# A two-layer token mixer on one core: order of work in the first phase of its recurrent part, and one gate tile moved to phase 8

## The reference

```python
xn = layernorm(x)
h = xn @ Win.T + bin                             # 512 -> 64 features
for l in range(4):
    y = silu(layernorm(h) * l1w + l1b)
    h = h + sconv(y) * scl                       # decaying complex recurrence over the 1024 tokens
    y = layernorm(h) * l2w + l2b
    h = h + silu(y @ W1.T + b1) @ W2.T + b2      # 64 -> 256 -> 64
s = layernorm(h) * lnw + lnb, then @ Wout.T + bout  # 64 -> 512
g = silu(xn @ W.T + bias + low-rank updates)     # 512 -> 512, folded into one matrix weff
x = x + s * g
```

## Time and profile before

| | us |
|---|---|
| median of 3 runs (lowest to highest) | 686.53 (683.98 to 686.88) |
| the profiled execution, its time | 686.92 |
| its span, first to last instruction | 684.8 |
| block A, to the start of block B | 470.3 |
| phase 0, to TensorE's first `center_rows` | 41.4 |
| phases 1 to 7 | 131.8 |
| phases 8 and 9, to the end of the span | 41.3 |

### The profile page before, as it was taken

The page is one execution under the profiler, slowest core; times in us unless marked ns, Lnnn a source line. Parts: engine busy times, 40 slices in busy tenths (PEclk is TensorE's granted clock), DMA queues, the critical chain, the costliest instruction groups (busy, mean ns, idle before and its releaser), DMA issues. The chain is left out here.

```text
span 684.8 us, 8597 instructions
## 1 busy us (share of the span) xinstructions
PE 626.5 (91%) x2772; PEld 450.5 (66%) x2772; DVE 489.6 (71%) x943; ACT 324.1 (47%) x541; POOL 171.9 (25%) x296
## 2 busy tenths in 40 slices
PE   4797999999999999999999999898499999999785
PEld 4676878888888888888888888466244343434332
DVE  6798897787787787787887877587574544445556
ACT  5679286277277267357357448222233333333420
POOL 1000002002002002001001006966543544443324
PEclk9999999999999999999999999899699999999977
DMA  8811001100100200200200107202000000000014
GB/s 296 295 43 63 0 1 52 42 1 28 64 0 0 92 0 0 92 0 0 92 0 0 63 1 259 89 1 58 6 1 0 1 0 0 1 0 1 0 61 185
DMA packets 17182, 32.32 MB, mean 47 GB/s; under 512 B 3225, under 2 KB 3737, under 8 KB 17153
## 3 DMA queue, kind: packets, MB, share of 16 engines
q1 hardware_dynamic: 17152, 31.97, 13.6%
HBM read 24.62 MB, written 7.34 MB: 47 GB/s over the span
## 5 line engine op out<-in xcount | busy, mean ns | idle before, releaser
L750 DVE TENSOR_SCALAR_CACHE_REDUCE junk_d<-k_buf,cand 128x1376 int8<-128x1376 f32 x56 | 91.9, 1640 | 0.3
L581 ACT ACTIVATE junk_a<-k_buf,cand 128x1376 int8<-128x1376 f32 x56 | 80.5, 1437 | 0.6
L1014 PE MATMUL ps_a<-wd_hi,zt_hi 128*128 128x512 f32 (+1 forms) x176 | 71.8, 408 | 1.9 <-DVE zt_lo L863 1.0
L1729 PE MATMUL ps_b<-arena,xt 128*128 128x512 f32 x128 | 71.6, 670 | 0.0
L562 ACT ACTIVATE s_buf<-ps_a 128x1376 f32<-128x1376 f32 x16 | 21.1, 1320 | 106.0 <-PE ps_a L987 103.6
L1014 PE MATMUL ps_a<-wd_hi,zt_lo 128*128 128x512 f32 (+1 forms) x176 | 69.2, 393 | 0.0
L1014 PE MATMUL ps_a<-wd_lo,zt_hi 128*128 128x512 f32 (+1 forms) x176 | 68.9, 392 | 0.0
L503 POOL TENSOR_TENSOR xres<-xres,gate 128x512 f32<-128x512 f32 x12 | 23.5, 1962 | 144.4 <-DVE gate L870 144.4
L495 POOL TENSOR_TENSOR rstd<-var_eps,expo 128x2 f32<-128x2 f32 x8 | 5.6, 706 | 203.7 <-DVE var_eps L691 203.7
L987 PE MATMUL ps_a<-wg_hi,xt_hi 128*128 128x512 f32 (+1 forms) x192 | 52.7, 383 | 1.8 <-DVE xt_lo L679 1.8
L987 PE MATMUL ps_b<-wu_hi,xt_hi 128*128 128x512 f32 (+1 forms) x192 | 52.3, 381 | 0.0
(11 more groups left out here) (225 smaller groups left out, 1282.6 us busy)
## 6 DMA issues: line engine op xcount, KB each, us to landing
xin<-in_x SPq DMA_DIRECT2D x8, 512.0 KB, 3.7
xres<-in_x SPq DMA_DIRECT2D x8, 512.0 KB, 3.4
out<-arena SPq DMA_DIRECT2D x16, 256.0 KB, 2.0
x_scratch<-xres SPq DMA_DIRECT2D x6, 512.0 KB, 3.1
arena<-x_scratch SPq DMA_DIRECT2D x3, 1024.0 KB, 11.8
m_buf<-in_wd_t SPq DMA_DIRECT2D x3, 512.0 KB, 9.3
m_buf<-in_wg_t SPq DMA_DIRECT2D x2, 688.0 KB, 5.6
k_buf<-in_wg_t SPq DMA_DIRECT2D x2, 688.0 KB, 8.0
```

The costliest lines, as they stand in the source:

```text
L581: act.activation(junk_a[:], k_buf[:, 1, :], ACT.Sign, bias=c, scale=-1.0, accum_out=below[:, 1:2]).then_inc(act_step, 1)
L750: dve.tensor_scalar(junk_d[:], k_buf[:, 0, :], c, -float(DROP), ALU.is_lt, ALU.add, accum_out=e).then_inc(cnt_dve, 1)
L1014: last = pe.matmul(ps_a[:, t, :], zs, ws[0:rows, c, :], start=(c == 0 and n == 0), stop=(c == CHUNKS - 1 and n == 2))
L1729: last = pe.matmul(bankg[k % 2], xt[:, n - 1, t * P:(t + 1) * P], weff[:, n - 1, :], start=False, stop=(n == KH))
```

## The change

On ScalarE, `apply_tokens` now normalizes groups 2 and 3, as scale and bias of an activation; VectorE makes the bias (`negated`, minus mean times inverse root) and normalizes no tile of block B. Six banks serve for the transposes. The statistics of group 3 stand between VectorE's copies. The low part of the bias rows is made for two rows alone, in waits of VectorE (`rows_low`), and the means of `w2` are taken in a wait (`weight_means`), apart from their subtraction (`take_means`). GpSimd takes the first inverse roots ahead of its constants, and makes three tables of a phase instead of two, the third after `widen`. The bias row of a gate tile becomes its last step. In phase 0 one gate tile is made instead of two, and the sixteenth tile lies in phase 8 (`LAST_GATES`). In each phase ScalarE's `gate` of the first tile moves behind both `norm_out`s.

```diff
+LAST_GATES = (0, 1, 2, 2, 0, 0)
...
+            nmr = sb("nmr", [P, 8])
...
+            TOKEN_BANK = (0, 1, 2, 3, 4, 5, 0, 1, 4, 5, 0, 1, 5, 0, 1, 5)
+
             def token_bank(i):
-                return xbank[i % 4] if i < 12 else bankx[i % 2]
+
+
+                return (bankx + bankg + [bank1[1], bank2[1]])[TOKEN_BANK[i]]
+
+            def takes_on_vector(i):
+                return i < PER_HALF and i % 2 == 1
+
+            def taken(i):
+                return sum(takes_on_vector(j) == takes_on_vector(i) for j in range(i + 1))
...
-                pool.memset(row_f[:], 0.0).then_inc(rows_zero, 1)
-                make(pool.memset(expo2[:], -0.5))
...
+                make(pool.memset(expo2[:], -0.5))
                 root_tokens(2)
-                tables_some(0, 6)
+                pool.memset(row_f[:], 0.0).then_inc(rows_zero, 1)
+                make(pool.memset(center[:], 0.0))
...
+                tables_some(0, 3)
                 root_tokens(3)
+                tables_some(3, 6)
+                root(0, 0)
+                pool.wait_ge(ln_w[0], 1)
                 tables_some(6, 8)
-                root(0, 0)
-                tables_some(8, 10)
-                pool.wait_ge(tb, N_SMALL + 6)
                 times_sin(0, 0, y, ln_o, 1, cv_wi)
                 times_sin(0, 0, u_im, cv_ui, 1, cv_b)
-                pool.wait_ge(h_ready[0], 2)
-                tables_some(10, 14)
                 for phase in range(1, PHASES):
                     l, c = mixing(phase)
                     k, d = feeding(phase)
                     feeds = phase < PHASES - 1
-                    if phase > 1 and l < DEPTH:
-                        pool.wait_ge(h_ready[c], 2 * l + 1)
-                        tables_some(10 + 2 * phase, 12 + 2 * phase)
+                    if l < DEPTH:
+                        if phase == 1:
+                            pool.wait_ge(h_ready[0], 2)
+                        else:
+                            pool.wait_ge(h_ready[c], 2 * l + 1)
+                        tables_some(5 + 3 * phase, 7 + 3 * phase)
                     root(2 * l, c)
                     if feeds:
                         root(2 * k + 1, d)
+                    if l < DEPTH:
+                        pool.wait_ge(ln_w[d], 2 * k + 2)
+                        tables_some(7 + 3 * phase, 8 + 3 * phase)
...
+                def apply_tokens(i):
+
+                    act.wait_ge(nmr_s, i - 1)
+                    for j in range(4):
+                        m = 4 * i + j
+                        act.activation(xn_tile(m), x1[:, 4 * ORDER[i] + j, :], ACT.Identity,
+                                       scale=rs2[:, m:m + 1], bias=nmr[:, m - 8:m - 7]).then_inc(xn_s, 1)
+
                 for i in range(0, PER_HALF, 2):
                     take_tile(i)
+                apply_tokens(2)
                 act.wait_ge(rows_in, 16 * 8)
                 act.activation(row_r[:], row_f[:], ACT.Copy).then_inc(rows_hi, 1)
                 act.wait_ge(mk, N_MK)
                 act.activation(ones_r[:], ones[:], ACT.Copy).then_inc(rows_lo, 1)
-                act.wait_ge(rows_left, 1)
-                for r in (32, 96):
-                    act.activation(row_r[r:r + 1, :, :], row_f[r:r + 1, :, :], ACT.Copy).then_inc(rows_lo, 1)
                 squares(0, 0)
+                apply_tokens(3)
                 for i in range(PER_HALF, PER_HALF + 4):
                     take_tile(i)
...
                 gate(0)
-                gate(1)
                 for phase in range(1, PHASES):
                     l, c = mixing(phase)
                     k, d = feeding(phase)
...
                     if l < DEPTH:
-                        gate(2 * phase)
                         norm_out(q, c, ACT.Silu, pcol(l, C_L1W), pcol(l, C_L1B))
                     else:
                         norm_out(q, c, ACT.Identity, par_last[:, 0:1], par_last[:, 1:2])
                     if feeds:
                         norm_out(n, d, ACT.Identity, pcol(k, C_L2W), pcol(k, C_L2B))
+                        gate(2 * phase - 1)
                         if phase == 1:
                             act.wait_ge(last_in, 16 * N_LAST)
                         for u in range(4):
                             hidden(k, d, u)
                             if u == 2 and l < DEPTH:
-                                gate(2 * phase + 1)
+                                gate(2 * phase)
...
-                def apply_tokens(i):
+                def negated(i):
+
+                    w = slice(4 * i, 4 * i + 4)
                     dve.wait_ge(root2, i - 1)
-                    norm2_apply(dve, i)
+                    dve.scalar_tensor_tensor(out=nmr[:, 4 * i - 8:4 * i - 4], in0=mv2[:, w, 0], scalar=-1.0,
+                                             in1=rs2[:, w], op0=ALU.mult, op1=ALU.mult).then_inc(nmr_s, 1)
+
+                def rows_low(r):
+                    dve.wait_ge(rows_hi, 1)
+                    dve.tensor_tensor(row_r[r:r + 1, :, :], row_f[r:r + 1, :, :],
+                                      row_r[r:r + 1, :, :].bitcast(F32), ALU.subtract).then_inc(rows_lo, 1)
...
-                def center_weights(w, at, n, loaded, count, done):
+                def weight_means(w, at, n, loaded, count, done):
...
+
+                def take_means(w, at, n, done):
+                    mean = off[:, at:at + n]
...
-                def token_stats(j0, j1):
+                def token_stats(j):
                     dve.wait_ge(x1_ready, TILES)
-                    for j in range(j0, j1):
-                        dve.bn_stats(stats2[:, 12 + j, :], x1[:, 4 * ORDER[3] + j, :]).then_inc(st2, 1)
-                    for j in range(j0, j1):
+                    dve.bn_stats(stats2[:, 12 + j, :], x1[:, 4 * ORDER[3] + j, :]).then_inc(st2, 1)
+
+                def token_means():
+                    for j in range(4):
                         dve.wait_ge(st2, 12 + j + 1)
                         dve.bn_aggr(mv2[:, 12 + j, :], stats2[:, 12 + j, :]).then_inc(mv2_s, 1)
 
                 add_eps(2)
-                center_weights(win, 0, KH, win_in, 16, win_s)
-                for i in (1, 3, 5, 7):
-                    take_tile(i)
-                dve.wait_ge(rows_hi, 1)
-                dve.tensor_tensor(row_f[:], row_f[:], row_r[:].bitcast(F32), ALU.subtract).then_inc(rows_left, 1)
-                apply_tokens(2)
+                weight_means(win, 0, KH, win_in, 16, win_s)
+                take_means(win, 0, KH, win_s)
+                take_tile(1)
+                take_tile(3)
+                negated(2)
+                token_stats(0)
+                take_tile(5)
+                take_tile(7)
+                for j in range(1, 4):
+                    token_stats(j)
+                token_means()
+                add_eps(3)
                 dve.wait_ge(bc_ps, 1)
                 dve.tensor_copy(bias_c[:], bank2[0][:, 0:DEPTH + 1]).then_inc(bc_s, 1)
                 dve.wait_ge(bc_s, 1)
                 h_in(0)
-                token_stats(0, 2)
+                negated(3)
+                rows_low(32)
                 variance(0, 0)
-                token_stats(2, 4)
-                add_eps(3)
+                rows_low(96)
                 widen(0, 0)
                 normed(0, 0)
-                apply_tokens(3)
+                weight_means(w2[:], KH, 2 * DEPTH, w2_in, 16, w2_s)
                 dve.wait_ge(rho_s, 1)
                 for phase in range(PHASES):
                     l, c = mixing(phase)
@@ -1657,18 +1696,15 @@
                                 residual(m - 1)
                         residual(TILES - 1)
                     if phase == 0:
-                        center_weights(w2[:], KH, 2 * DEPTH, w2_in, 16, w2_s)
                         h_in(1)
+                        take_means(w2[:], KH, 2 * DEPTH, w2_s)
...
-                    if 4 <= i < 8:
-                        pe.wait_ge(xt_v if i % 2 else xt_a, i // 2 - 1)
-                    elif 8 <= i < 12:
-                        pe.wait_ge(xt_v if i % 2 else xt_a, i // 2 - 1)
-                    elif i >= 12:
-                        pe.wait_ge(xt_a, i - 7 if i < 14 else i - 5)
+                    held = [j for j in range(i) if TOKEN_BANK[j] == TOKEN_BANK[i]]
+                    if held:
+                        pe.wait_ge(xt_v if takes_on_vector(held[-1]) else xt_a, taken(held[-1]))
...
-                    if n == 0:
-                        if k >= 2:
-                            pe.wait_ge(g_done, k - 1)
-                        pe.matmul(bankg[k % 2], ones_r[0:DIM, :], row_r[0:DIM, 0, :], start=True, stop=False)
+                    if n == 0 and k >= 2:
+                        pe.wait_ge(g_done, k - 1)
+                    if n < KH:
+                        pe.matmul(bankg[k % 2], xt[:, n, t * P:(t + 1) * P], weff[:, n, :],
+                                  start=(n == 0), stop=False)
                         return
```

(58 more changed lines are left out.)

## The result

The changed kernel took 657.46 us in the median (656.31 to 658.63, 4 runs), the kernel before 685.25 beside it. The ratio is 0.960, with an interval of 0.958 to 0.962. The profiled execution took 658.63, with a span of 656.8. The forecast was 665.6, in 660.5 to 672.5: the direction was right, and the gain of 27.8 us lies above the range, where 20.9 was forecast.

What follows compares the result with a forecast made beforehand. It took phase 0 as bound by a VectorE and GpSimd chain, phases 1 to 7 by TensorE with a hole before up_unit. −14.7 − 5.4 − 0.8 = −20.9 gave a median of 665.6 us, range 660.5 to 672.5.

Steps and rivals of the forecast that it cites:

- Phase 0: Start of block B, a chain through VectorE and GpSimd: −14.7 us, bounds −12.5 to −15.6.
- phase 8: Gains 4.1 us of gate work, mostly in TensorE's idle pieces: −0.8 us, between +1.2 and −2.5.
- Phases 1 to 7: TensorE sets the pace; hole −4.3 and widen waits −1.1: sum −5.4 us, bounds −2.5 to −9.
- step 8: Phase 0, TensorE: its work ends near 496.5 or 497.5; center_rows of phase 1 at 497.0 instead of 511.68.
- step 4: Phase 0, GpSimd: group 3 roots near 479.3, three more tables in 4.5 us, root(0,0) at 484.8 instead of 492.06.
- The hole: TensorE's wait before up_unit in phases 1 to 7, from ScalarE's order, goes: −4.3 us in seven pieces.
- the −1.1 for the waits before the `spread`s: Phases 1 to 7: TensorE comes later to the first spread, so waits for widen shrink by 1.1 us.
- 4 × 0.9 of the bound: Phases 1 to 7: saved if no phase has a fall to 1.2 GHz; a bound, outside the sum.
- GpSimd's table and root did grow: Rival: tables and roots grow beside VectorE's two-input operations; phase 0 gains 10, not 14.7: 670 us. Chance 0.12.
- No row load was late: Rival: ScalarE waits for late bias rows in phase 0, eating all gains if 21 us after 480. Chance 0.02.
- no filled hole took the gain away: Rival: only phase 0 gains; another wait fills the hole, the moved tile costs 4.1: 675 us. Chance 0.10.
- The clock stays up: Rival: the clock stays up in the phases and phase 8, 3 to 5 us more gain: 662 us. Chance 0.10.

Runs made afterwards that it cites:

- tokens_vector: The changed kernel with both groups of block B normalized on VectorE again and without the small negations: 659.55 us.
- tile_early: The changed kernel with the sixteenth gate tile back in phase 0, behind project_in(1), and none in phase 8: 661.17 us.
- before_shift2: The kernel before with two more unread products directly ahead of phase 1: 685.00 us.
- before_bias_last: The kernel before with the bias row as the last step of a gate tile, alone: 675.11 us.
- before_gate_behind: The kernel before with ScalarE's activation of the first gate tile behind both norm_outs in phases 1 to 7, alone: 678.21 us.
- first_empty: The changed kernel with GATES (0, 3, 1, 3, 2, 1), so the product ahead of the narrow matmuls stands behind them: 665.65 us.
- shift2: The changed kernel with two more unread products ahead of phase 1: 658.23 us.
- tables_and_rows: The changed kernel with rows_low(96) and weight_means exchanged, and one table ahead of a phase's roots and two behind widen: 657.07 us.

## Why the prediction was right and where it was wrong

The median of 657.46 lies below the range of 660.5 to 672.5. Phase 0 and phase 8 came out near their forecasts; the miss is in phases 1 to 7.

**Phase 0 was right, by its own steps.** `h_in(0)` came at 479.75 (forecast 480.2, with block A 0.5 earlier), `turn` at 489.25 (490.2), `center_rows` at 496.68 (497.0). Four normalizations on ScalarE took 2.92 (3.3), the rows were in before they were asked for, and `project_in(1)` and `into_h` ended within 0.1 of each other, as step 8 had them. In part this is luck, as two errors cancelled. The roots of group 3 started a us sooner than in step 4, since GpSimd had waited 0.27 and not 1.1 for the first variances. `rows_low` took 1.99 twice, near the upper bound, and the third table took 2.03 and `root(0,0)` 2.63 beside it, so that the root ended at 486.31 where 484.8 + 1.64 = 486.4 had been forecast. The removed piece of 4.43 us was a misleading price, though: the normalizations' move is worth 2.9 (tokens_vector), the tile 4.0 (tile_early), and the rest of the 14.5, about 7.6, belongs to what they don't touch, the order of statistics, roots, tables and weight means. That rest was not split further.

**The failing step is "Phases 1 to 7", its sum of −5.4.** It measured −11.8. Three things:

- "The first place of `GATES` now holds a product in place of the bias row, 0.5 longer": the same exchange made the sixth place 0.5 shorter, on the path, and the step left that term out. 0.49 × 7 = 3.4.
- The hole was priced at 0.61 by the wait; from start to start it was 0.69, 4.8 in all. Against that the −1.1 for the waits before the `spread`s did not come: they grew from 1.5 to 2.6, and the second `spread` is where it was. Only phase 6, with one table ahead of its roots in place of two, is 0.4 shorter again.
- The clock was left at four falls, as a bound and not in the sum, and they went. Against a phase of the kernel before without a fall (18.51), phases 3 and 5 were 0.7 and 0.6 longer. Phase 7, with no table ahead of its roots, was 19.25 against 17.94 in before_shift2, 1.3 longer. No run has phase 1 of the old order without a fall; before_bias_last has phases 1 and 7 alike (17.15 and 17.16), so I take 17.94 for it too, and its fall at 1.0, an estimate. That makes 3.6, just the 4 × 0.9 of the bound.

3.4 + 4.8 + 0.4 + 3.6 = 12.2. Phases 1, 4 and 7 gained 1.0 each by the order and not 1.18, as the kernel before had them shorter already (phase 4 was 18.30): 0.5 less, 11.7 for 11.8. The mechanism that the step gave to the hole, ScalarE's order, is right: before_gate_behind does that alone, and its first `up_unit` starts 0.69 sooner.

**Phase 8** came near (−1.2 for −0.8), by two terms of about a us against each other. `up_unit` came 10.65 after its start against 9.62 before, so the tile's steps cost 1.0 there, on a clock that had fallen after the narrow matmuls (four instructions took 2.61). But the clock was back by then, as the forecast had hoped: `up_unit`s took 1.13 against 2.08. How far the clock comes back moves this stage more than the forecast's whole term: with the gate tile in it, phases 8 and 9 took 38.8 to 39.1 in the three profiles with a granted clock of 1.00 in their first 19 us (first_empty, shift2, tables_and_rows), 39.9 to 40.4 at 0.91, and 41.9 to 42.1 at 0.82.

**The rivals.** GpSimd's table and root did grow, by 0.8 and 1.0, but its earlier start made up for it in phase 0. No row load was late, and no filled hole took the gain away. "The clock stays up" was the one that came, in phases 1 to 7, at the price given (3.6 of its 3 to 5). But it lay beside a main case that was itself about 3 us short.

**What stays open.** In all profiles of the table with a wait of at most 0.20 the clock did not fall in phases 2 to 7; in all with 0.33 or more it fell in two to four of phases 1 to 7. But all profiles of the first kind have one and the same order of steps up to the first `spread`: one product ahead of the narrow matmuls and two behind. No run has this order with a longer wait there, or another order with a wait as short. More waiting did not bring more falls, and phase 7 of the kernel before fell, though the same phase has no wait ahead of its `spread` where it does not fall (before_shift2). So the wait marks the orders that fall, but what the chip judges, and whether it is the wait or something that goes with it, is not shown. In windows of phase 0 the granted clock was 0.51 of full speed where TensorE was busy for 2.51 us of ten, and 0.83 where it was for 8.18. The Trainium skill (TensorE: Matmul & The Clock Gate, The HAM clock gate) ties the clock to how busy the array has been; these windows agree in the direction.

## What to carry to other kernels

When a fixed piece of work is reordered over numbered places, write down the change of every place: one that gets longer inside a wait costs nothing, and the one that gets shorter on the path is the gain. Let a result end with its shortest step if another engine waits for it and holds up the path: that was worth 0.44 us a phase, and nothing once ScalarE's order had taken `y` from behind it. Try each of two edits alone before sharing a gain out between them, since their parts need not add up. Where narrow matmuls stand beside a wait, look at the granted clock phase by phase: here orders that differ in the place of one step had none or two to four falls, of 0.6 to 1.7 us each in phases 2 to 7.

## What the runs showed of the hardware

- A VectorE subtraction of 1 × 1024 with two inputs from SBUF took 1.99 us where a GpSimd table was under way, and 1.22 where it started first and the table took 2.06 in place of 1.27 (tokens_vector). GpSimd's root took 2.63 beside it and 1.64 behind it (tokens_vector). `rows_low(96)` ended at 484.80, 1.1 after the table ended at 483.72; the root ended at 486.31, 1.5 after that. Each seems to have waited for the other in full. The Trainium skill (SBUF — State Buffer, SBUF: two separate sides) says that a VectorE instruction with two inputs in SBUF and a GpSimd instruction that reads SBUF need the same pair of ports, and that whichever starts first holds it for its whole length while the other waits; these rows agree.
- A bias row of 64 partitions right behind `up_unit`s of 64 partitions started 0.03 us after the last of them did, at 527.52 against 527.49. The pair, the bias row and the `down_unit`s took 3.97, of which 3.40 is what the other two take where a product stands between them (1.06 and 2.34, phase 2 of the kernel before): it cost 0.57, and not less than its 0.43.
- The clock fell in two of six like phases and not in the others, with the same instructions of TensorE in the same order (phases 4 and 7 of first_empty, 19.31, against 17.62 or 17.63 in phases 2, 3, 5 and 6).
